# Transposing products of rotated q and k placed one by one between the products with v, and the maxima transposed as fp32r

## The chip, the cores and the metric

The kernel runs on one core of a Trainium2 chip. The metric is the device time of one execution in microseconds. TensorE is written PE, VectorE DVE, ScalarE ACT, GpSimd POOL, SyncE SP, as in the profile; PEld are PE's weight loads.

## The reference, cut to what matters

The kernel is one transformer layer on 16 batch elements of 256 tokens by 128 features: modulated layer norm, attention with 16 query heads, 4 key and value heads and rotary embedding, a residual, then a second modulated layer norm and a two-layer MLP with binarized weights.

```python
h = _layernorm(x) * (1 + ca) + sa
q = (h @ Wq)  -> 16 heads of 64;  k, v = h @ Wkv -> 4 heads of 64
q = q * cos + _rotate_half(q) * sin        # k alike
attn = softmax(q @ k.T * SCALE)
x = x + ga * (attn @ v @ Wo + bo)
h = _layernorm(x) * (1 + cb) + sb
return x + gb * (gelu(h @ bw1 + b1) @ bw2 + b2)
```

## The kernel before, in words

**Stages.** A prologue loads weights and prepares modulation and signs. Then come 18 attention steps (`attention_steps`, L129): one that only prepares, one per batch element, and a tail; then the MLP steps (`mlp_steps`, L143). In an attention step of the steady kind, of which there are 14 (batch elements 1 to 14), three batch elements are in hand: the attention of this one, the output product of the one before, and the normalisation, q, k, v and rotation of the next.

**Slots.** A step has eight slots, one per pair of heads. In each slot PE makes the transposed scores of the pair (`scores`, L942, two chunks of keys, here S0 and S1, two products of 512 columns each), and the product of the previous pair's probabilities with v (`product_with_v`, L958): six products of 512 columns, of high and low parts, in four parts of 2, 2, 1 and 1. Between these stand *units*, listed by hand in `UNITS` (L60) and dealt out one after each S and each part (`slot_order`, L180); what is left over comes at the end of the slot.

**Units.** "xT": transposes of the normalised tokens (2). "qkv c n": 512 columns of q, k, v for token chunk c, three products; n = 2 is k and v, n = 0 and 1 are q. "kt", "qt": the rotated k or q of two heads transposed, four products of 128 columns against an fp32r identity (L907). "s h": row-wise scores of head h, two products of 256 columns, only for the maxima. "mT": the maxima of four heads transposed in fp32. "bc": the reciprocal sums of a pair broadcast to 64 rows each, one product of 256 columns. "yT": the output product, eight fp32 products, in two halves. "zT": back to token rows.

**Who reads a unit.** DVE reads s (the maxima, L728), bc (normalises the pair's output into `o_t`, two instructions, L733), qkv (v_lo at L712, then the two rotation products rot_a and rot_b at L718 and L720), zT (L738); it also makes the low part of the layer norm output from xT (h_lo, L704). ACT reads xT (h_t, h_hi), the v part of qkv (v_hi, L541), kt, qt, mT and yT, and makes the exponentials, two for each S. Rotation goes on from DVE to POOL (rot_sum, L468), ACT (L570) and POOL again (L472).

**Order and waits.** Each engine runs its own list of instructions strictly in order, and every list goes through the units in the same order, `slot_order`. So moving a unit moves its reader's place too, if the units around it have the same reader. DVE has work of its own at fixed slots: statistics ahead of slot 4, normalising ahead of slot 6, the reciprocals of the sums ahead of slots 2 and 5 (L743), and the low part of the probabilities of pairs 0, 2 and 6 at the end of their slots (L827). The units share four PSUM banks in turn (`unit_banks`, L79): a unit waits until the unit four places before it, of the same bank, has been read (`wait_for_reader`, L853).

**The reciprocals.** DVE makes reciprocals with a high and a low part (L746 to L750), SP sends both with two DMAs (L407), and the first bc of the half waits for both to land (L927). The bc of pairs 4 to 7 belong to the batch element before and stand in slots 3 and 4.

Of the kernel before, what the change touches and what calls it, by code (L numbers as in the profile page):

```python
# [178 lines left out]

def slot_order(st, s):  # L180

    held = {"scores": st.attn, "pv": st.attn if s >= 1 else st.out, "un": st.attn if s >= 2 else st.out}
    rest, order = units(st, s), []
    for w in WORK:
        if held[w[0]]:
            order.append((None, w))
            if rest and w[0] in ("scores", "pv"):
                order.append(rest.pop(0))
    return order + rest
# [43 lines left out]
def adaln_layer(nc, x, wq, wkv, wo, bo, w1, b1, w2, b2, c, wmod, cos, sin, out):  # L233
    ctx = ExitStack()
    with ctx:
# [129 lines left out]
        def _(sp):  # L365
            sp.dma_start(c_sb[:, :], c).then_inc(c_in, 16)
            sp.dma_start(xa[:, 0, :, :], x[0].rearrange("(c p) d -> p c d", p=P)).then_inc(x0_in, 16)
            sp.dma_start(wmod_sb[:, :], wmod).then_inc(wmod_in, 16)
# [725 lines left out]
```

## Time and profile before

| | |
|---|---|
| median of 3 runs | 766.95 us (766.94 to 767.4) |
| the profiled execution | 766.3 us, span 764.5 us |
| PE busy | 677.3 us (89%), 3829 instructions |
| DVE busy | 607.1 us (79%), 1275 instructions |
| ACT busy | 592.2 us (77%) |
| POOL busy | 539.4 us (71%) |
| granted TensorE clock, mean | 0.962 |

Times in the rows are microseconds from the span's start. A timeline row gives the start, the length, engine, line, operation, output and inputs; in square brackets the idle time of the engine before it and what ended that. PE's products are pipelined: a row's length holds the fill of the array, so what a product costs is read from the distance between ends of successive rows. The granted clock is 1.00 from 66 to 663 us, which is the upper level, 2.4 GHz.

### The profile page before, as it was taken

How to read it: one execution, taken by the hardware profiler on the slowest of the kernel's cores; microseconds unless marked ns; L12 is line 12 of the kernel's file. 1: busy time of each engine (PE TensorE's matmuls, PEld its weight loads, DVE VectorE, ACT ScalarE, POOL GpSimd, SP SyncE). 2: the span in 40 equal slices, each digit the busy share in tenths (PEclk: the TensorE clock that was granted, in tenths of full speed). 3: DMA queues.
4: the chain of work that ended last, by engine and by line, in shares of the span. 5: the costliest groups of instructions: out<-in, count | busy, mean ns of one | idle time of the engine just before them, and what ended most of it. 6: DMA issues, size and time to landing. Idle time of an engine off the chain costs nothing.

```text
span 764.5 us, 14217 instructions
## 1 busy us (share of the span) xinstructions
PE 677.3 (89%) x3829; PEld 541.3 (71%) x3829; DVE 607.1 (79%) x1275; ACT 592.2 (77%) x1213; POOL 539.4 (71%) x459
## 2 busy tenths in 40 slices
PE   3588999999999999999999999999999999866665
PEld 3465787868777778777777777777778787655654
DVE  6767878787878787888878787878787878549995
ACT  2578988888888888888889888888888888626664
POOL 1568787868696969696877878687878786505564
PEclk9599999999999999999999999999999999978888
DMA  8011111110101111111111101111111111000001
GB/s 234 14 29 30 30 31 30 31 28 18 40 16 28 29 29 29 29 29 29 29 29 29 26 19 29 29 29 29 29 30 30 30 30 30 16 1 17 25 27 42
DMA packets 31578, 24.72 MB, mean 32 GB/s; under 512 B 16688, under 2 KB 26944, under 8 KB 31552
## 3 DMA queue, kind: packets, MB, share of 16 engines
q1 hardware_dynamic: 31552, 24.40, 14.7%
q8 instruction: 13, 0.21, 0.1%
q14 instruction: 13, 0.11, 0.0%
HBM read 4.47 MB, written 2.10 MB: 9 GB/s over the span
## 4 chain that ended last, share of the span: by engine, by line
PE 44%; DVE 21%; issue 18%; ACT 8%; POOL 5%; DMA 1%; DVEq 1%; SPq 0%; POOLq 0%; ACTq 0%
PE o_ps L977 10%; PE unit_ps L934 8%; DVE w_all L728 4%; DVE o_t L733 4%; PE score_ps L952 4%; PE score_ps L954 4%; PE unit_ps L907 4%; PE unit_ps L918 4%; POOL probs_lo L483 3%; DVE recip_hi L748 2%; DVE rot_a L718 2%; DVE rot_b L720 1%; PE unit_ps L928 1%; POOL rot_sum L468 1%; PE unit_ps L891 1%
## 5 line engine op out<-in xcount | busy, mean ns | idle before, releaser
L483 POOL TENSOR_TENSOR probs_lo<-probs,probs_hi 128x512 fp32r<-128x512 f32 x208 | 270.8, 1314 | 51.9 <-ACT probs_hi L622 50.6
L468 POOL TENSOR_TENSOR rot_sum<-rot_a,rot_b 128x512 f32<-128x512 f32 (+1 forms) x96 | 113.2, 1179 | 109.2 <-DVE rot_b L720 108.9
L728 DVE TENSOR_REDUCE w_all<-unit_ps 128x2 f32<-128x512 f32 x256 | 166.4, 683 | 7.9 <-PE unit_ps L918 6.7
L620 ACT ACTIVATE probs<-score_ps 128x512 f32<-128x512 f32 x256 | 150.9, 589 | 3.5 <-PE score_ps L954 3.2
L622 ACT ACTIVATE probs_hi<-score_ps 128x512 fp32r<-128x512 f32 x256 | 152.2, 594 | 0.0
L918 PEld LDWEIGHTS unit_ps<-k_hi,q_hilo 128*128 128x128 f32 x512 | 95.1, 193 | 37.9 <-DVE o_t L733 6.0
L907 PEld LDWEIGHTS unit_ps<-ident_r,qk_rot 128*128 128x128 f32 x640 | 95.7, 194 | 29.4 <-DVE o_t L733 13.3
L733 DVE TENSOR_TENSOR o_t<-o_un,unit_ps 64x256 f32<-64x256 f32 x256 | 106.8, 417 | 8.5 <-PE unit_ps L928 3.8
L952 PE MATMUL score_ps<-q_hilo,k_hi 128*128 128x512 f32 x256 | 108.1, 422 | 2.9 <-DMA q_him<-neg_max_t 1.5
L472 POOL TENSOR_TENSOR qk_rot<-rot_sum,qk_rot 128x512 fp32r<-128x512 f32 (+1 forms) x96 | 105.6, 1106 | 5.2 <-ACT qk_rot L570 5.2
L918 PE MATMUL unit_ps<-k_hi,q_hilo 128*128 128x256 f32 x512 | 106.1, 291 | 2.7 <-DVE rot_b L720 1.4
L907 PE MATMUL unit_ps<-ident_r,qk_rot 128*128 128x128 f32 x640 | 92.7, 269 | 10.9 <-DVE o_t L733 9.0
L977 PE MATMUL o_ps<-probs_lo,v_hi 128*65 128x512 f32 x256 | 101.5, 405 | 0.0
L954 PE MATMUL score_ps<-q_him,k_lo 65*128 65x512 f32 x256 | 101.5, 397 | 0.0
L552 ACT ACTIVATE q_hilo<-unit_ps 128x512 fp32r<-128x512 f32 x128 | 74.3, 595 | 23.2 <-PE unit_ps L907 22.2
L977 PE MATMUL o_ps<-probs_hi,v_hi 128*65 128x512 f32 x256 | 80.2, 394 | 0.0
L977 PE MATMUL o_ps<-probs_hi,v_lo 128*65 128x512 f32 x256 | 79.8, 393 | 0.0
L627 ACT ACTIVATE o_un<-o_ps 65x512 f32<-65x512 f32 x128 | 74.7, 584 | 3.9 <-PE o_ps L977 2.3
L718 DVE TENSOR_TENSOR rot_a<-unit_ps,cos_sb 128x512 f32<-128x512 f32 (+1 forms) x96 | 57.3, 597 | 18.9 <-PE unit_ps L893 18.1
L934 PEld LDWEIGHTS unit_ps<-o_t,wo_sb 128*128 128x128 f32 x512 | 62.6, 196 | 11.0 <-DVE o_t L733 9.6
L934 PE MATMUL unit_ps<-o_t,wo_sb 128*128 128x128 f32 x512 | 65.1, 282 | 4.6 <-DVE o_t L733 4.6
L455 POOL TENSOR_TENSOR rstd<-var_eps,minus_half 128x2 f32<-128x2 f32 x32 | 27.2, 850 | 48.0 <-DVE var_eps L660 48.0
(110 smaller groups left out, 1206.4 us busy)
## 6 DMA issues: line engine op xcount, KB each, us to landing
q_him<-q_hilo SPq DMA_DIRECT2D x64, 256.0 KB
out_x<-w_all SPq DMA_DIRECT2D x16, 128.0 KB, 1.8
xa<-in_L_attn_x SPq DMA_DIRECT2D x3, 640.0 KB, 6.9
q_him<-neg_max_t SPq DMA_DIRECT2D x64, 4.0 KB
w_all<-in_L_attn_Wq SPq DMA_DIRECT2D x1, 512.0 KB, 4.2
w_sb<-in_L_ffn_w SPq DMA_DIRECT2D x2, 256.0 KB, 3.1
wo_sb<-in_L_attn_Wo SPq DMA_DIRECT2D x1, 512.0 KB, 7.5
sums<-o_un SPq DMA_DIRECT2D x32, 8.0 KB, 2.0
```

What stands on the lines that cost most here:

```text
L468: pool.tensor_tensor(total, rot_a[k % 2][:, 0:heads, :], rot_b[k % 2][:, 0:heads, :], ALU.add).then_inc(rot_summed, 1)
L483: pool.tensor_tensor(probs_lo[s % 2][:, jc, :, :], probs[s % 2][:, jc, :, :], probs_hi[s % 2][:, jc, :, :].bitcast(F32), ALU.subtract).the ...
L620: act.activation(probs[s % 2][:, jc, :, :].rearrange("p h i -> p (h i)"), score_ps[jc][:, :], ACT.Exp, scale=SCALE)
L622: act.activation(probs_hi[s % 2][:, jc, :, :].rearrange("p h i -> p (h i)"), score_ps[jc][:, :], ACT.Exp, scale=SCALE).then_inc(probs_read ...
L728: dve.tensor_reduce(neg_max[u[1] // 4][:, first:first + C], ps[:, :].rearrange("p (c j) -> p c j", c=C), AX.X, ALU.max, negate=True).then_ ...
L733: ins = dve.tensor_tensor(o_t[h * DH:h * DH + DH, u[1], :], o_un[0:DH, u[1], h, :], ps[h * DH:h * DH + DH, 0:N], ALU.mult)
L907: ins = pe.matmul(ps[:, h * N + ch * P:h * N + (ch + 1) * P], qk_rot[:, ch, first + h, :, :].rearrange("p t d -> p (t d)"), ident_r[:, :], ...
L918: ins = pe.matmul(ps[:, ch * N:(ch + 1) * N], q_hilo[par][:, h, ch * P:(ch + 1) * P], k_hi2[par][:, g, :], start=True, stop=True)
L934: ins = pe.matmul(ps[:, own], wo_sb[:, s, :], o_t[:, s, own], start=s == 0, stop=s == PAIRS - 1)
L952: pe.matmul(ps[:, :], k_hi2[par][:, g, js], q_hilo[par][:, hs, :].rearrange("p h i -> p (h i)"), start=True, stop=False)
L954: pe.matmul(ps[:, :], k_lo1[par][:, g, js], q_him[s // 2 % 2][:, s % 2 * 2:s % 2 * 2 + 2, :].rearrange("p h i -> p (h i)"), start=False, s ...
L977: ins = pe.matmul(o_ps[i][0:DH + 1, :], v[par][:, jc, g, :], p[i][:, jc, :, :].rearrange("p h i -> p (h i)"), start=part == 0 and jc == 0, ...
```

## The change

`UNITS` is replaced by `SLOTS`, which writes out every slot in full: S0, S1 are the scores, "m" is one single product with v, and a kt, qt, xT or zT stands once for each of its products. The four products of a kt or qt thus stand one by one, most of them each behind an m. The order of the units changes with it; an evicting engine takes a unit at the place of its last product. The maxima get a tile of their own in fp32r, and are transposed by a product with the fp32r identity. `wmod_sb` moves into the memory of `probs[1]`.

```diff
-UNITS = [
-    [("s", 4), ("s", 5), ("s", 6), ("s", 7), ("xT", 0), ("qt", 4), ("mT", 1)],
-    [("qkv", 0, 2), ("s", 8), ("qkv", 1, 2), ("qt", 5), ("s", 9)],
-    [("s", 10), ("s", 11), ("qkv", 0, 0), ("qt", 6), ("mT", 2)],
-    [("s", 12), ("qkv", 1, 0), ("bc", 4), ("bc", 5), ("kt", 0), ("qt", 7)],
-    [("bc", 6), ("bc", 7), ("s", 13), ("s", 14), ("s", 15), ("yT", 0), ("mT", 3)],
-    [("yT", 1), ("kt", 1), ("qkv", 0, 1), ("qt", 0), ("qt", 1)],
-    [("s", 0), ("s", 1), ("s", 2), ("s", 3), ("qkv", 1, 1), ("mT", 0), ("zT", 0)],
-    [("bc", 0), ("bc", 1), ("bc", 2), ("qt", 2), ("qt", 3), ("bc", 3)],
+SLOTS = [
+    "S0 s4 S1 s5 m s6 m s7 m xT0 m xT0 m qt4 m qt4 qt4 qt4 mT1",
+    "S0 qkv02 S1 m qt5 m qt5 m qt5 m qt5 m s8 m qkv12 s9",
+    "S0 s10 S1 s11 m qt6 m qt6 m qt6 m qt6 m qkv00 m mT2",
+    "S0 bc4 S1 bc5 m qt7 m qt7 m qt7 m qt7 m s12 m qkv10",
+    "S0 bc6 S1 bc7 m s13 m kt0 m kt0 m kt0 m kt0 m s14 s15 yT0 mT3",
+    "S0 S1 yT1 m qt0 m qt0 m qt0 m qt0 m qt1 m qt1 qt1 qt1 qkv01",
+    "S0 s0 S1 s1 m s2 m s3 m kt1 m kt1 m kt1 m kt1 qkv11 zT0 zT0 mT0",
+    "S0 bc0 S1 bc1 m qt2 m qt2 m qt2 m qt2 m qt3 m qt3 qt3 qt3 bc2 bc3",
 ]
...
+        neg_max = sb("neg_max", [P, 4, P], F32R)
...
-        neg_max = [w_all[:, 2 * FF + i * P:2 * FF + (i + 1) * P] for i in range(4)]
+        wmod_sb = probs[1][:, :, :, :].rearrange("p c h i -> p (c h i)")[:, 0:6 * D]
...
-                    for h in range(2):
-                        for ch in range(C):
-                            ins = pe.matmul(ps[:, h * N + ch * P:h * N + (ch + 1) * P],
-                                            qk_rot[:, ch, first + h, :, :].rearrange("p t d -> p (t d)"),
-                                            ident_r[:, :], start=True, stop=True)
+                    h, ch = part // 2, part % 2
+                    ins = pe.matmul(ps[:, part * P:(part + 1) * P],
+                                    qk_rot[:, ch, first + h, :, :].rearrange("p t d -> p (t d)"),
+                                    ident_r[:, :], start=True, stop=True)
...
-                    ins = pe.transpose(ps[:, 0:P], neg_max[u[1]], ident[:, :])
+                    ins = pe.matmul(ps[:, 0:P], neg_max[:, u[1], :], ident_r[:, :], start=True, stop=True)
...
-                p, v, chunks = [(probs_hi, v_hi, (0, 1)), (probs_hi, v_lo, (0, 1)),
-                                (probs_lo, v_hi, (0,)), (probs_lo, v_hi, (1,))][part]
-                for jc in chunks:
-                    ins = pe.matmul(o_ps[i][0:DH + 1, :], v[par][:, jc, g, :], p[i][:, jc, :, :].rearrange("p h i -> p (h i)"),
-                                    start=part == 0 and jc == 0, stop=part == 3)
+                p, v = [(probs_hi, v_hi), (probs_hi, v_lo), (probs_lo, v_hi)][part // 2]
+                jc = part % 2
+                ins = pe.matmul(o_ps[i][0:DH + 1, :], v[par][:, jc, g, :], p[i][:, jc, :, :].rearrange("p h i -> p (h i)"),
+                                start=part == 0, stop=part == 5)
```

## Rows read from the trace of the kernel before

**Rows 1.** The page, busy time of each engine.

```profile
PE 677.3 (89%) x3829; PEld 541.3 (71%) x3829; DVE 607.1 (79%) x1275; ACT 592.2 (77%) x1213; POOL 539.4 (71%) x459
```

**Rows 2.** PE timeline about one qt (386.56), the window ending after one, two, four products.

```profile
386.32 0.40 PE L977 MATMUL o_ps<-probs_hi,v_lo 128*65 128x512 f32 x1
386.56 0.22 PE L907 MATMUL unit_ps<-ident_r,qk_rot 128*128 128x128 f32 x1
386.56 0.33 PE L907 MATMUL unit_ps<-ident_r,qk_rot 128*128 128x128 f32 x2
386.56 0.56 PE L907 MATMUL unit_ps<-ident_r,qk_rot 128*128 128x128 f32 x4
```

**Rows 3.** Busy time by stretch (length, PE, PEld, DVE, ACT, POOL, clock, DMA).

```profile
357.82:361.66 3.84, 3.84 (x25) 3.19 (x23) 3.75 (x8) 2.96 (x7) 2.84 (x3) 1.00 0.32 68
361.66:364.66 3.00, 2.54 (x12) 1.79 (x12) 1.03 (x3) 2.97 (x9) 0.00 (x0) 1.00 0.01 1
364.66:379.66 15.00, 14.76 (x80) 11.36 (x78) 14.63 (x33) 13.28 (x28) 13.66 (x13) 1.00 0.15 30
379.66:386.38 6.72, 6.57 (x48) 6.00 (x49) 2.49 (x7) 4.71 (x11) 5.66 (x6) 1.00 0.08 16
386.38:397.35 10.97, 10.35 (x58) 7.67 (x56) 10.55 (x17) 9.48 (x21) 8.77 (x7) 1.00 0.13 26
317.63:397.35 79.72, 76.16 (x437) 60.36 (x436) 65.18 (x131) 66.78 (x140) 61.81 (x53) 1.00 0.14 28
```

**Rows 4.** Waits of DVE in one step, 357.82 to 397.35 (total us, times, longest).

```profile
DVE recip L746 <- DMA sums<-o_un: 3.5, 1, 3.5
DVE v_lo L712 <- ACT v_hi L541: 1.2, 1, 1.2
DVE rot_a L718 <- PE unit_ps L893: 0.9, 2, 0.6
DVE h_lo L704 <- ACT h_hi L539: 0.7, 1, 0.7
```

**Rows 5.** DVE timeline, slots 1 to 3 of that step.

```profile
366.26 0.41 DVE L712 TENSOR_TENSOR v_lo<-unit_ps,v_hi 128x256 fp32r<-128x256 f32 x1
...
368.13 0.97 DVE L748 CAST recip_hi<-recip 128x16 fp32r<-128x16 f32 x1
369.13 0.66 DVE L750 TENSOR_TENSOR recip_lo<-recip,recip_hi 128x16 fp32r<-128x16 f32 x1
...
373.61 0.69 DVE L718 TENSOR_TENSOR rot_a<-unit_ps,cos_sb 128x512 f32<-128x512 f32 x1
```

**Rows 6.** ACT timeline, the second v_hi of slot 1.

```profile
365.80 0.38 ACT L541 ACTIVATE v_hi<-unit_ps 128x256 fp32r<-128x256 f32 x1 [0.21 <-PE unit_ps L893]
```

**Rows 7.** SP timeline, the reciprocals' second DMA of slot 2, and PE's first bc.

```profile
370.54 0.66 SPq L407 DMA_DIRECT2D recip_parts<-recip_lo  x1
...
373.79 0.28 PE L928 MATMUL unit_ps<-recip_parts,select 128*128 128x256 f32 x1
```

**Rows 8.** Timeline of the tail step, where nothing else covers the reciprocals.

```profile
672.48 0.17 DVE L748 CAST recip_hi<-recip 128x16 fp32r<-128x16 f32 x1
...
673.55 0.61 SPq L407 DMA_DIRECT2D recip_parts<-recip_lo  x1
675.51 0.47 PE L928 MATMUL unit_ps<-recip_parts,select 128*128 128x256 f32 x2 [2.48 <-DMA recip_parts<-recip_lo]
```

**Rows 9.** DVE timeline, slot 4.

```profile
377.93 1.73 DVE L733 TENSOR_TENSOR o_t<-o_un,unit_ps 64x256 f32<-64x256 f32 x4
379.70 1.89 DVE L728 TENSOR_REDUCE w_all<-unit_ps 128x2 f32<-128x512 f32 x3
```

**Rows 10.** PE timeline, slots 4 and 5.

```profile
379.81 2.02 PE L934 MATMUL unit_ps<-o_t,wo_sb 128*128 128x128 f32 x16 [0.23 <-DVE o_t L733]
381.67 0.30 PE L922 MATMUL unit_ps<-ident,w_all 128*128 128x128 f32 x1
...
384.54 0.56 PE L907 MATMUL unit_ps<-ident_r,qk_rot 128*128 128x128 f32 x4
...
385.86 0.40 PE L893 MATMUL unit_ps<-w_hi,h_lo 128*128 128x512 f32 x1
```

More of the change, by code:

```diff
@@ L48, with parsed @@
 EPS = 1e-5
-UNITS = [
[8 rows of a table removed]
-]
-ALL_UNITS = [(slot, u) for slot, units in enumerate(UNITS) for u in units]
+SLOTS = [
[8 rows of a table added]
+]
+def parsed(slots):
+    found = []
+    for text in slots:
+        words, slot, product = text.split(), [("un",)], 0
+        for n, word in enumerate(words):
+            kind = word.rstrip("0123456789")
+            number = word[len(kind):]
+            if kind == "S":
+                slot.append(("scores", int(number)))
+            elif kind == "m":
+                slot.append(("pv", product))
+                product += 1
+            else:
+                name = (kind, *map(int, number)) if kind == "qkv" else (kind, int(number))
+                slot.append(("part", name, words[:n].count(word), word not in words[n + 1:]))
+        found.append(slot)
+    return found
+ORDER = parsed(SLOTS)
+ALL_UNITS = [(slot, w[1]) for slot, order in enumerate(ORDER) for w in order if w[0] == "part" and w[3]]
+PLACE = {u: k for k, (_, u) in enumerate(ALL_UNITS)}
 LATE_UNITS = ([("qt", s) for s in range(4, PAIRS)] + [("s", h) for h in range(4, HEADS)] + [("mT", q) for q in range(1, 4)]
@@ L177, in units, with slot_parts @@
     return [(k, u) for k, (s, u) in enumerate(ALL_UNITS) if s == slot and has(st, u)]
+def slot_parts(st, s):
+    held = {"scores": st.attn, "pv": st.attn if s >= 1 else st.out, "un": st.attn if s >= 2 else st.out}
+    return [w for w in ORDER[s] if (has(st, w[1]) if w[0] == "part" else held[w[0]])]
 def slot_order(st, s):
[L182 to L189, printed above, removed]
+    return [(PLACE[w[1]], w[1]) if w[0] == "part" else (None, w)
+            for w in slot_parts(st, s) if w[0] != "part" or w[3]]
 def rotated(st, s, end):
@@ L367, in _ @@
             sp.dma_start(xa[:, 0, :, :], x[0].rearrange("(c p) d -> p c d", p=P)).then_inc(x0_in, 16)
[L368 removed]
+            sp.dma_start(wmod_sb, wmod).then_inc(wmod_in, 16)
             sp.dma_start(w_all[:, 0:INNER], wq).then_inc(wq_in, 16)
@@ L727, in unit @@
                     first = u[1] % 4 * C
-                    dve.tensor_reduce(neg_max[u[1] // 4][:, first:first + C], ps[:, :].rearrange("p (c j) -> p c j", c=C), AX.X,
+                    dve.tensor_reduce(neg_max[:, u[1] // 4, first:first + C], ps[:, :].rearrange("p (c j) -> p c j", c=C), AX.X,
                                       ALU.max, negate=True).then_inc(max_ready, 1)
@@ L873, in wait_for_reader, with unit @@
                     pe.wait_ge(x2_ready, st.count(1, 1, of))
-            def unit(st, place, u):
+            def unit(st, place, u, part, last):
                 kind, ps, par = u[0], unit_ps[bank(st, place)], st.par(ahead(u))
                 before = last_in_bank(st, place)
-                if before and u != ("yT", 1):
+                if before and u != ("yT", 1) and part == 0:
                     wait_for_reader(st, *before)
                 if kind == "xT":
-                    pe.wait_ge(ln_out, st.count(1, 1, 1))
-                    for ch in range(C):
-                        ins = pe.transpose(ps[:, ch * P:(ch + 1) * P], xn[:, ch, :], ident[:, :])
+                    if part == 0:
+                        pe.wait_ge(ln_out, st.count(1, 1, 1))
+                    ins = pe.transpose(ps[:, part * P:(part + 1) * P], xn[:, part, :], ident[:, :])
                 if kind == "qkv":
@@ L936, in unit @@
                 if kind == "zT":
-                    pe.wait_ge(z_ready, st.count(1, 1, -1))
-                    for ch in range(C):
-                        ins = pe.transpose(ps[:, ch * P:(ch + 1) * P], z_sb[:, ch * P:(ch + 1) * P], ident[:, :])
-                ins.then_inc(unit_full, 1)
+                    if part == 0:
+                        pe.wait_ge(z_ready, st.count(1, 1, -1))
+                    ins = pe.transpose(ps[:, part * P:(part + 1) * P], z_sb[:, part * P:(part + 1) * P], ident[:, :])
+                if last:
+                    ins.then_inc(unit_full, 1)
             def scores(st, s, jc):
@@ L1051, in step @@
                 for s in range(PAIRS):
-                    for place, w in slot_order(st, s):
-                        if place is not None:
-                            unit(st, place, w)
+                    for w in slot_parts(st, s):
+                        if w[0] == "part":
+                            unit(st, PLACE[w[1]], *w[1:])
                         elif w[0] == "scores":
```

22 lines of the change are left out of this document (9 added, 13 removed).

## The prediction

> **What bounds the kernel now.** The page's busy times come first: PE 677.3 us of 764.5, DVE 607.1, with PEld at 541.3 [rows 1]. By that PE is the bound, and work taken off it should come off the time. The second view asks whether this holds inside a step. Two steady steps take 79.72 us, 39.86 each, and PE counts 76.16 of them as busy [rows 3]; but a busy row holds the fill of the array, so short stalls hide in it. DVE's busy time does not hide stalls. I cut one step at DVE's waits [rows 4] into four legs [rows 3], and read who holds whom:
>
> - Leg 1, 361.66 to 364.66, 3.00 us: DVE is done with the maxima of slot 0 and waits until layer norm, ACT's exponentials and v_hi of slot 1 are through.
> - Leg 2, 364.66 to 379.66, 15.00 us: slots 1 to 4. DVE is busy for 14.63 of it.
> - Leg 3, 379.66 to 386.38, 6.72 us: from the last bc read to the rotation of qkv01. DVE does 2.49 us of work; PE makes yT0, yT1 and qkv01.
> - Leg 4, 386.38 to 397.35 and on through the 3.84 us ahead of leg 1 (357.82 to 361.66), 14.81 us: slots 5 to 7 and slot 0. DVE is busy for 10.55 of 10.97 and 3.75 of 3.84.
>
> The four sum to 39.53, this step without the loop's branch. So DVE is the bound over 29.8 us of a step, through its strict order of work, and PE and ACT bound it only where they hand DVE the next piece: leg 1, leg 3, and the short wait ahead of qkv11 (the 0.9 us in two parts, the longest 0.6, of [rows 4]). What the change does to these hand-overs decides.
>
> **What it takes from PE.** In a group of four the first product ends 0.06 us after the long product before it (386.72 to 386.78), each later one 0.11 later: four end 0.40 after it [rows 2]. The later ones wait for their own weights; the first's were loaded under 512 columns. A lone product between two m should cost 0.06, four 0.24. Six groups of a step stand quite alone (qt5, qt6, qt7, kt0, qt0, qt2): 6 x 0.15; kt1's last is followed by qkv11, whose 128 columns of weights it can't hide: 0.10; qt4, qt1 and qt3 gain by the first only: 3 x 0.05. Sum 1.15 us a step. The maxima as fp32r: the transpose now ends 0.14 after yT0's last product (379.81 + 2.02 to 381.67 + 0.30 [rows 10]); the shorter one still stands ahead of S0, whose weights then show instead. I put it at nothing, within 0.05 x 4 either way.
>
> Here I weigh a rule. The Trainium skill, "TensorE: Matmul & The Clock Gate", part 3, "The mechanism", says that a weight load overlaps a running product only where it goes to other rows of the array. By it a lone product would cost its load as well, 0.11 as now, and the 1.15 would be nothing; the 0.06 in [rows 2] says otherwise, and I take the row.
>
> **What it does to the legs.** All prices are for one step; a 512-column product costs 0.23 (two between 386.26 [rows 10] and 386.72 [rows 2]), one of 256 half that.
>
> Leg 1. xT's second product stands behind four m instead of five: 0.23 earlier, and h_lo, qkv02 and v_hi with it: -0.23.
>
> Leg 2, first part. qkv12 stood behind S1, s8 and two m; now behind S1, six m, the four qt5 and s8. That is 4 x 0.23 + 0.24 = 1.16 later against qkv02. Its v_hi on ACT already waited for PE by 0.21 [rows 6], and DVE took v_lo as soon as s8 was done (366.26 [rows 5]), with about 0.07 to spare. So v_lo comes 1.1 later: +1.1. Behind it in DVE's list are s9, the reciprocals, s10, s11: all of slot 2 follows, and mT2, now the very last of slot 2, waits for s11's maximum and holds S0 of slot 3.
>
> Leg 2, second part. Before, DVE went from the end of recip_lo (369.79 [rows 5]) through s10, s11, qkv00, the low part and s12 to rot_a of qkv10 at 373.61: 3.82 us, and the landing of the reciprocals was covered, since bc4 came at 373.79, behind qkv10 [rows 7]. Now bc4 is the second thing in slot 3. The tail step shows the bare landing: 1.96 from the issue of the second DMA to PE's bc (673.55 to 675.51 [rows 8]). From recip_lo's end to that issue are 0.75 (369.79 to 370.54 [rows 5, 7]), so bc4 ends 0.75 + 1.96 + 0.36 = 3.07 after recip_lo. PE would be there after 2.2 (s10 and s11 on DVE 1.2, mT2 0.4, S0 and bc4 0.6): a new wait of 0.9. Queued behind it on PE are S1, bc5, six m, qt7, s12 and qkv10: 0.46 + 0.12 + 1.40 + 0.24 + 0.23 + 0.70 = 3.15, and DVE's rot_a another 0.13 later (385.86 + 0.40 to 386.38, [rows 10, 3]). So rot_a starts 6.35 after recip_lo instead of 3.82; but bc4 and bc5, four o_t instructions or 1.73 [rows 9], are by then done, which stood behind it: 6.35 - 3.82 - 1.73 = +0.8.
>
> Leg 3. Two things. yT0 takes the bank of s13, which DVE reads only after bc7; before, its bank was bc7's own. It starts one maximum later, 1.89 / 3 = 0.63, with the step to the first of them 0.7 [rows 9]: +0.7. And qkv01, before which S0, yT1, S1, kt1 and two m stood, is now last: six m, qt0 (0.24) and qt1 (0.06 + 0.28, its three in a row and the load of qkv01's weights) stand before it instead of two m and kt1 (0.40 [rows 10]): 4 x 0.23 + 0.24 + 0.34 + 0.05 - 0.40 = +1.15. DVE has nothing else to do meanwhile (2.49 of 6.72 busy).
>
> Leg 4. DVE's order is the same. kt1 now waits for the reader of s0, which costs PE but not DVE; qkv11 comes a bit before DVE is ready instead of 0.33 after: -0.15. bc2 and bc3 wait for DVE at the end as qt3 and bc3 did.
>
> Other queues: SP's order is unchanged; its DMAs for q and for the maxima of quarter 0 are issued with some 4 us to their use, as before. POOL's order is unchanged, and it has 8 us a step to spare [rows 3]. ACT takes kt0 a slot later and z behind S1's exponentials; neither is waited for longer than DVE's chain.
>
> **The sum.** -0.23 + 1.1 + 0.8 + 0.7 + 1.15 - 0.15 = +3.4 us a step. 14 steps: +47.6. The preparing step, step 0 and step 15 have parts of it (step 0 the two late qkv, 2.2): +3, between 0 and 6. Against the profiled execution of 766.3 us that is 816.9, and the median of the runs, 766.95, lies 0.65 above it: **817 us**.
>
> Bounds. Below: the cast of the reciprocals takes 0.97 and recip_lo 0.66 in the steady step [rows 5], the cast 0.17 in the tail [rows 8], where POOL is idle; if they fall between POOL's instructions, leg 2 loses up to 1.3. If the landing is as short as to be covered, 0.9 more. Then 1.2 a step: 784. Above: lone products at 0.11 add 0.05 for each of the 13 in legs 2 and 3, 0.65, and new collisions of the kind of those two 0.6: 4.65 a step, 837.
>
> **Rivals.**
>
> *PE is the bound after all* (other side). DVE's full stretches would then be slack taken up by PE's pace: units come earlier, DVE starts earlier, and each step gives 1.15. For it: 89% against 79% [rows 1], and PE's waits are short. Against it: DVE's 10.55 of 10.97, in the leg where it would have to start earlier. It decides at qkv01: if DVE's wait ahead of that rotation does not grow by more than PE's gain. 14 x 1.15 = 16: 750.8, say 751. Chance 0.16.
>
> *Lone products don't hide their loads* (the rule above, as a mechanism here): all legs as in my sum, with the 0.65 of the upper bound: 14 x 0.65 = 9 more, 826. The first product of each group in [rows 2] speaks against it. Chance 0.07.
>
> *Only the two late qkv cost.* bc4's landing and s13's bank are covered by DVE's own shift: -0.23 + 1.1 + 1.15 - 0.15 less PE's 1.15: 0.7 a step, 777. Chance 0.06.
>
> *Gain and waits cancel*, the maxima and lone products leaving the time as it is: 767. Chance 0.05.
>
> My forecast: 0.66. **Numbers.** About 0.2% of the time is what a measurement of this kernel tells from no change. Slower: 0.66 + 0.07 + 0.06 = 0.79; same 0.05; faster 0.16. The range goes from 766, which takes in the rivals above and the no-change case, to 837: it leaves out the faster case and some 0.04 beyond its ends.
>
> **What would show it.** In the changed kernel a step should be about 43 us long; DVE's wait for qkv01's rotation should be near 2 us instead of 0.6; a wait of the second v_lo on v_hi of some 0.6 should be new, and one of PE's bc in slot 3 on the reciprocals' DMA of 0.9; yT0 should wait on a maximum (L728), not on o_t; lone fp32r transposes should end 0.06 after the m before them, and PEld's busy time stay as it is. The prediction is wrong if the step is below 39.8, if bc4 never waits on the DMA, or if DVE reaches s0 of slot 6 no later after yT1 than now.

## The result and the profile after

The changed kernel takes 839.64 us (median of 4 runs, 836.8 to 841.01) against 767.17 us before (the median of now 4 runs): a ratio of 1.0932, 95% interval 1.0907 to 1.0957. The direction was forecast; the size was not: 817 us was predicted, and the time lies 2.6 us above the range's upper end of 837. The profiled execution took 836.8 us, span 834.9 us, against a span of 764.5 us.

In the new kernel's line numbers the maxima are L748, o_t L753, the reciprocals L766 to L770, rot_a and rot_b L738 and L740, v_lo L732, kt and qt L926, s L937, mT L941, bc L947, yT L953, qkv L911 to L913, the scores S0 and S1 L972 and L974, the products with v L996. First the page: busy time of each engine and the granted clock in 40 slices; the last row is the clock of the kernel before.

```profile
PE 691.4 (83%) x3829; PEld 558.3 (67%) x3829; DVE 617.5 (74%) x1275; ACT 595.1 (71%) x1213; POOL 534.8 (64%) x459
...
PEclk9789899999999999999999999999999999978886
...
PEclk9599999999999999999999999999999999978888
```

No engine came nearer to being the bound than in [rows 1]: PE fell from 89% to 83%. From the sixth slice on the clock's row is 9 through all the steps, as it was before, because a short fall is lost in a slice of 21 us. The next view, busy time by stretch (columns as in [rows 3]), shows one step cut at the prediction's four legs, then the whole of that step, a second step's leg 3, and the 13 steps in which all marks can be read.

```profile
309.15:311.94 2.79, 2.58 (x12) 1.80 (x12) 1.03 (x3) 2.78 (x8) 0.00 (x0) 1.00 0.01 1
311.94:329.14 17.20, 14.17 (x79) 11.00 (x77) 14.99 (x33) 13.39 (x28) 14.89 (x14) 1.00 0.16 32
329.14:337.65 8.51, 8.23 (x58) 7.42 (x59) 3.27 (x7) 5.35 (x12) 5.21 (x5) 1.00 0.01 1
337.65:352.33 14.68, 12.53 (x71) 9.79 (x70) 14.16 (x24) 11.44 (x24) 10.45 (x8) 1.00 0.18 37
309.15:352.33 43.18, 37.51 (x216) 30.01 (x216) 33.45 (x66) 32.96 (x69) 30.54 (x26) 1.00 0.13 26
...
417.69:427.83 10.14, 9.87 (x58) 9.05 (x59) 3.24 (x6) 5.34 (x12) 5.20 (x5) 0.83 0.01 1
...
85.89:666.22 580.33, 507.50 (x2838) 407.71 (x2836) 435.02 (x845) 437.15 (x899) 397.06 (x338) 0.97 0.12 25
```

The first step is the one that the prediction described: 2.79, 17.20, 8.51, 14.68 against 3.00, 15.00, 6.72, 14.81 in [rows 3], so -0.21, +2.20, +1.79, -0.13; forecast were -0.23, +1.9, +1.85, -0.15. It is 43.18 long, 3.65 more than before, where 3.4 was forecast. But the 13 steps take 580.33 us, 44.64 each, and their mean granted clock is 0.97. The row of 10.14 shows the difference: the same leg 3 with the same instructions, at a clock of 0.83. The same 13 steps of the kernel before, 39.80 each:

```profile
82.62:600.00 517.38, 494.70 (x2837) 392.44 (x2836) 423.01 (x846) 434.63 (x898) 401.78 (x339) 1.00 0.14 28
```

The waits of the undisturbed step (309.15 to 352.33; total us, times, longest) are those named in the forecast:

```profile
DVE recip L766 <- DMA sums<-o_un: 4.1, 1, 4.1
...
DVE v_lo L732 <- ACT v_hi L562: 1.9, 2, 1.2
DVE rot_a L738 <- PE unit_ps L913: 1.7, 3, 1.0
...
PE unit_ps L941 <- DVE neg_max L748: 1.4, 1, 1.4
...
PE unit_ps L947 <- DMA recip_parts<-recip_lo: 0.7, 1, 0.7
...
PE unit_ps L953 <- DVE neg_max L748: 0.2, 1, 0.2
```

v_lo now waits twice, bc4 waits for its DMA, yT0 for a maximum. mT2's wait of 1.4 for s11's maximum is the longest stand of PE in the step. Behind it and bc4's wait lies what the forecast lacked. Busy time by stretch of another step, slots 2 and 3:

```profile
494.46:496.80 2.34, 2.34 (x14) 1.59 (x12) 2.27 (x4) 2.29 (x6) 2.34 (x3) 1.00 0.00 0
496.80:500.60 3.80, 1.78 (x8) 1.29 (x9) 3.63 (x8) 1.78 (x5) 2.66 (x4) 0.98 0.05 5
500.60:504.01 3.41, 3.41 (x14) 2.85 (x13) 1.53 (x4) 2.12 (x4) 3.41 (x4) 0.52 0.00 0
504.01:510.00 5.99, 4.83 (x26) 3.58 (x25) 5.29 (x15) 4.96 (x9) 4.56 (x5) 1.00 0.21 44
```

PE is busy throughout, then for 1.78 of 3.80 us; then its clock is 0.52, the lower level of 1.2 GHz, for 3.41 us, and full again. PE's timeline of slot 3 in the undisturbed step (322) and in this one (501):

```profile
321.87 0.40 PE L996 MATMUL o_ps<-probs_hi,v_hi 128*65 128x512 f32 x1
322.11 0.22 PE L926 MATMUL unit_ps<-ident_r,qk_rot 128*128 128x128 f32 x1
322.17 0.39 PE L996 MATMUL o_ps<-probs_hi,v_hi 128*65 128x512 f32 x1
...
501.46 0.63 PE L996 MATMUL o_ps<-probs_hi,v_lo 128*65 128x512 f32 x1
501.88 0.31 PE L926 MATMUL unit_ps<-ident_r,qk_rot 128*128 128x128 f32 x1
501.99 0.63 PE L996 MATMUL o_ps<-probs_hi,v_lo 128*65 128x512 f32 x1
```

At full clock the lone transposing product ends 0.06 after the product with v (322.27 to 322.33), as forecast, and the next product with v 0.23 later. At half clock the same distances are 0.10 (502.09 to 502.19) and 0.43 (to 502.62). Such a stretch at half clock is called a fall from here on. Ten falls, 37.5 us of half clock in all, lie in the 13 steps of the new kernel, each in another step: seven in leg 2 and three early in leg 3. Nine last 3.41 us and one, in the first of the 13 steps, 6.83. The kernel before has none between 45 and 669 us.

### The profile page after: what moved, and what is told of

Its sections match the earlier page's. It is cut to its first block, busy times and chain, and to the rows that moved or that the text cites. A ratio compares the mean times of both kernels' runs of the same rounds, so it can differ in the third digit from the quotient of the medians.

```text
span 834.9 us, 14265 instructions
## 1 busy us (share of the span) xinstructions
PE 691.4 (83%) x3829; PEld 558.3 (67%) x3829; DVE 617.5 (74%) x1275; ACT 595.1 (71%) x1213; POOL 534.8 (64%) x459
## 4 chain that ended last, share of the span: by engine, by line
PE 50%; DVE 23%; issue 11%; ACT 6%; DMA 4%; POOL 3%; SPq 1%; DVEq 1%; ACTq 0%; POOLq 0%
PE o_ps L996 14%; PE unit_ps L953 8%; DVE o_t L753 5%; DVE neg_max L748 4%; PE unit_ps L926 4%; PE score_ps L972 4%; DMA recip_parts<-recip_lo 4%; PE score_ps L974 3%; PE unit_ps L947 3%; PE unit_ps L937 3%; PE unit_ps L911 2%; DVE rot_b L740 2%; DVE recip_lo L770 2%; DVE xn L687 2%; PE unit_ps L913 2%
## 5 line engine op out<-in xcount | busy, mean ns | idle before, releaser
L504 POOL TENSOR_TENSOR probs_lo<-probs,probs_hi 128x512 fp32r<-128x512 f32 x208 | 267.7, 1302 | 53.4 <-ACT probs_hi L643 51.4
L748 DVE TENSOR_REDUCE neg_max<-unit_ps 128x2 fp32r<-128x512 f32 x256 | 163.2, 683 | 28.7 <-PE unit_ps L937 27.8
L926 PE MATMUL unit_ps<-ident_r,qk_rot 128*128 128x128 f32 x640 | 136.5, 243 | 19.1 <-DVE neg_max L748 16.1
L926 PEld LDWEIGHTS unit_ps<-ident_r,qk_rot 128*128 128x128 f32 x640 | 121.4, 200 | 31.3 <-DVE neg_max L748 21.8
L937 PEld LDWEIGHTS unit_ps<-k_hi,q_hilo 128*128 128x128 f32 x512 | 94.7, 192 | 39.4 <-DVE o_t L753 21.6
L937 PE MATMUL unit_ps<-k_hi,q_hilo 128*128 128x256 f32 x512 | 105.8, 291 | 15.5 <-DVE o_t L753 14.3
L753 DVE TENSOR_TENSOR o_t<-o_un,unit_ps 64x256 f32<-64x256 f32 x256 | 106.9, 417 | 13.2 <-PE unit_ps L947 8.4
L972 PE MATMUL score_ps<-q_hilo,k_hi 128*128 128x512 f32 x256 | 107.7, 421 | 2.2 <-issue 1.4
L974 PE MATMUL score_ps<-q_him,k_lo 65*128 65x512 f32 x256 | 103.3, 404 | 0.0
L996 PE MATMUL o_ps<-probs_hi,v_hi 128*65 128x512 f32 x256 | 97.5, 413 | 0.0
L996 PE MATMUL o_ps<-probs_lo,v_hi 128*65 128x512 f32 x256 | 95.3, 406 | 0.0
L996 PE MATMUL o_ps<-probs_hi,v_lo 128*65 128x512 f32 x256 | 93.1, 412 | 0.0
L738 DVE TENSOR_TENSOR rot_a<-unit_ps,cos_sb 128x512 f32<-128x512 f32 (+1 forms) x96 | 57.3, 597 | 31.5 <-PE unit_ps L913 31.5
L953 PE MATMUL unit_ps<-o_t,wo_sb 128*128 128x128 f32 x512 | 70.4, 296 | 4.4 <-DVE neg_max L748 3.1
L953 PEld LDWEIGHTS unit_ps<-o_t,wo_sb 128*128 128x128 f32 x512 | 67.1, 209 | 8.8 <-DVE neg_max L748 6.0
L591 ACT ACTIVATE qk_rot<-rot_sum 128x512 fp32r<-128x512 f32 (+1 forms) x96 | 52.4, 564 | 19.8 <-POOL rot_sum L489 19.8
```

The costliest lines, as they stand in the source:

```text
L504: pool.tensor_tensor(probs_lo[s % 2][:, jc, :, :], probs[s % 2][:, jc, :, :], probs_hi[s % 2][:, jc, :, :].bitcast(F32), ALU.subtract).the ...
L748: dve.tensor_reduce(neg_max[:, u[1] // 4, first:first + C], ps[:, :].rearrange("p (c j) -> p c j", c=C), AX.X, ALU.max, negate=True).then_ ...
L753: ins = dve.tensor_tensor(o_t[h * DH:h * DH + DH, u[1], :], o_un[0:DH, u[1], h, :], ps[h * DH:h * DH + DH, 0:N], ALU.mult)
L926: ins = pe.matmul(ps[:, part * P:(part + 1) * P], qk_rot[:, ch, first + h, :, :].rearrange("p t d -> p (t d)"), ident_r[:, :], start=True, ...
L937: ins = pe.matmul(ps[:, ch * N:(ch + 1) * N], q_hilo[par][:, h, ch * P:(ch + 1) * P], k_hi2[par][:, g, :], start=True, stop=True)
L953: ins = pe.matmul(ps[:, own], wo_sb[:, s, :], o_t[:, s, own], start=s == 0, stop=s == PAIRS - 1)
```

## The experiments

All are the changed kernel with other lines in `SLOTS`, save one. The table gives the mean of 13 steps, cut at the same marks on DVE's timeline; "full clock" is the mean of the steps without a fall, and "falls" counts the stretches at half clock in the 13 steps. "Full clock" rests on few steps where falls are many: three in the changed kernel and in qkv01 early, one in kt0 in slot 3. (Steps are of two kinds that take turns, with a leg 1 of 2.8 or 3.3 us in the changed kernel.) The ratio is to runs of the kernel before that were taken along with each kernel; their medians lie between 767.17 and 768.98 us. The kernels stand in the order in which they are told; two more orders follow at the end.

| kernel | us | ratio to before (95%) | legs 1, 2, 3, 4 | step | full clock | falls |
|---|---|---|---|---|---|---|
| before | 767.17 | | 3.18, 15.02, 6.71, 14.89 | 39.80 | 39.80 | 0 |
| changed | 839.64 | 1.0932 (1.0907 to 1.0957) | 3.04, 18.06, 8.88, 14.66 | 44.64 | 43.40 | 10 |
| old order | 768.79 | 0.9977 (0.9942 to 1.0012) | 3.18, 15.02, 6.76, 15.00 | 39.96 | 39.85 | 1 |
| old order, lone products | 770.60 | 1.0034 (1.0017 to 1.0051) | 3.03, 15.03, 6.76, 14.82 | 39.64 | 39.64 | 0 |
| new order, groups | 837.88 | 1.0858 (1.0784 to 1.0933) | 3.02, 18.19, 8.84, 14.26 | 44.32 | 43.31 | 9 |
| filled | 830.71 | 1.0813 (1.0770 to 1.0855) | 3.04, 17.74, 8.51, 14.66 | 43.94 | 43.94 | 0 |
| slot 3 old | 807.08 | 1.0459 (1.0386 to 1.0531) | 3.04, 16.49, 8.50, 14.66 | 42.69 | 42.26 | 4 |
| qkv12 early | 821.75 | 1.0663 (1.0623 to 1.0703) | 3.04, 16.16, 9.37, 14.65 | 43.23 | 42.27 | 7 |
| qkv01 early | 822.24 | 1.0675 (1.0641 to 1.0710) | 3.05, 18.40, 7.59, 14.66 | 43.70 | 42.56 | 10 |
| kt0 first | 839.41 | 1.0920 (1.0901 to 1.0938) | 3.05, 17.46, 9.37, 14.65 | 44.52 | 43.49 | 9 |
| kt0 in slot 3 | 830.10 | 1.0774 (1.0729 to 1.0819) | 3.05, 18.53, 7.92, 14.65 | 44.15 | 42.56 | 12 |
| all hand-overs | 812.47 | 1.0546 (1.0470 to 1.0622) | 3.04, 15.03, 9.45, 15.13 | 42.65 | 41.38 | 9 |

**Is it the order, or the products and the tile?** The first kernel keeps the fp32r maxima, their tile and the single products in the list, but writes out the order of before, the groups of four together:

```diff
-    "S0 bc4 S1 bc5 m qt7 m qt7 m qt7 m qt7 m s12 m qkv10",
+    "S0 s12 S1 qkv10 m m bc4 m m bc5 m kt0 kt0 kt0 kt0 m qt7 qt7 qt7 qt7",
...
-    "S0 S1 yT1 m qt0 m qt0 m qt0 m qt0 m qt1 m qt1 qt1 qt1 qkv01",
+    "S0 yT1 S1 kt1 kt1 kt1 kt1 m m qkv01 m m qt0 qt0 qt0 qt0 m qt1 qt1 qt1 qt1 m",
```

> The changed kernel with every unit back at its old place, kt and qt in fours, the products with v grouped as before; what stays of the change is the fp32r transpose of the maxima with its own tile, and the weights' place. Theory (the order of the units is what costs): 767 us, within 2 of the kernel before, a step of 39.9 us, granted clock 1.00. Rival (the fp32r maxima or the moved tiles cost something): above 775. Rival (they gain): below 763.

Measured: 768.79 us, the time of before; its step by stretch (columns as in [rows 3]):

```profile
202.26:205.29 3.03, 2.58 (x12) 1.83 (x12) 1.03 (x3) 3.00 (x9) 0.00 (x0) 1.00 0.01 1
205.29:220.27 14.98, 14.74 (x80) 11.34 (x78) 14.59 (x33) 13.27 (x28) 13.63 (x13) 1.00 0.15 30
220.27:227.02 6.75, 6.60 (x48) 6.04 (x49) 2.50 (x7) 4.71 (x11) 5.67 (x6) 1.00 0.09 18
227.02:242.07 15.05, 14.16 (x81) 10.88 (x79) 14.52 (x24) 12.09 (x26) 11.62 (x9) 1.00 0.18 36
```

So the fp32r maxima and the tile are worth nothing that can be measured, and the loss comes from the order of the list; the lone products, which this kernel takes out as well, are settled by the next two. One of its 13 steps has a fall, in leg 4, which is 16.57 there instead of 15.05: the order of before can draw one too.

The second puts the transposing products one by one into that old order of units; only products with v change their place for it:

```diff
-    "S0 bc0 S1 bc1 m m bc2 m m qt2 qt2 qt2 qt2 m qt3 qt3 qt3 qt3 m bc3",
+    "S0 bc0 S1 bc1 m bc2 m qt2 m qt2 m qt2 m qt2 m qt3 qt3 qt3 qt3 bc3",
```

> The old order of units in every slot, with kt and qt products alone behind an m wherever the order leaves one (17 of the 40 in a step stay behind another). Theory (DVE's list is the bound; lone products save only on PE's stretch from yT0 to qkv11): 0.2 to 0.4 us a step, 761 to 765; granted clock 1.00 in every step. Rival (PE is the bound): 0.9 us a step, 754. Rival (lone products cost something by themselves, as the run with all four hand-overs mended could also be read): above 775.

Measured: 770.6 us, above the 761 to 765 expected. The step is 39.64 instead of 39.80 and no more, though the clock stays up, and nearly all of that is leg 1 (3.18 to 3.03), where xT's second product stands behind one product less with v: the time that lone products save on PE is time that nobody waits for. The rival by which PE is the bound falls with that, and so does my hope of a faster kernel; the 2 us that the 13 steps gain are lost again before and behind them, and what loses them there I have not found.

The third is the mirror of that: the new order with the products in groups of four.

```diff
-    "S0 bc4 S1 bc5 m qt7 m qt7 m qt7 m qt7 m s12 m qkv10",
+    "S0 bc4 S1 bc5 m m m m qt7 qt7 qt7 qt7 m s12 m qkv10",
```

> The changed kernel's order of units, but each kt and qt again as four products in a row, standing where the last of its four stood, with the m ahead of them. Theory (order costs, lone products save PE a little): not faster than the changed kernel, 838 to 860, since 0.15 us per group comes back on the two hand-over legs. Rival (lone products between long ones are what slows PE or takes its clock down): the time falls towards 770, and the granted clock is 1.00 in every step.

Measured: 837.88 us with 9 falls. Lone products are neither the cost nor the cause of the falls.

**Do the falls come from PE standing still?** This kernel keeps the order of the changed one to the letter and gives PE dummy products where it waits:

```diff
+                if st.attn and part == 0 and u in (("s", 14), ("s", 15), ("yT", 0)):
+                    pe.wait_ge(o_un_ready, st.count(8, 3))
+                    for _ in range(3 if u == ("s", 14) else 2):
+                        pe.matmul(o_ps[0][:, :], w_hi[:, 0:P], w_hi[:, 0:512], start=True, stop=True)
...
+                    if u[1] == 2:
+                        for _ in range(8):
+                            pe.matmul(ps[:, P:512], w_hi[:, 0:P], w_hi[:, 0:384], start=True, stop=True)
...
+                    if u[1] == 4 and not st.tail:
+                        for _ in range(6):
+                            pe.matmul(ps[:, N:512], w_hi[:, 0:P], w_hi[:, 0:N], start=True, stop=True)
```

> The changed kernel in its own order, with TensorE given dummy products where it stands still: eight of 384 columns ahead of mT2's wait for s11's maximum, six of 256 ahead of the first bc's wait for the reciprocals' DMA, and three, two and two of 512 ahead of s14, s15 and yT0. They go to unused columns or to an accumulator that is overwritten afterwards, and nothing reads them. Theory (the granted clock falls because TensorE stands still in short pieces at the new waits): the clock is 1.00 through the steady steps, a step is about 43.5 us with legs of 3.06, 17.3, 8.5 and 14.7, and the time falls although TensorE has more work: 820 to 826 us. Rival (the falls come from something else in the new order, such as the mix of short products): the falls to half stay, a step is 44.6 us or longer, 836 to 845 us.

Measured: 830.71 us. Its legs 2 and 3 in one step, and its 13 steps (columns as in [rows 3]):

```profile
308.98:326.68 17.70, 16.90 (x98) 13.89 (x96) 14.90 (x33) 13.37 (x28) 14.99 (x14) 1.00 0.15 31
326.68:335.20 8.52, 8.52 (x61) 7.65 (x61) 3.26 (x7) 5.35 (x12) 5.26 (x5) 1.00 0.01 1
...
85.93:657.20 571.27, 530.22 (x3111) 434.39 (x3109) 434.18 (x845) 435.20 (x899) 398.77 (x338) 1.00 0.13 26
```

All ten falls are gone, and every step has a leg 3 of 8.4 to 8.5, though PE now counts 530 us as busy where it had 507. So the falls hang on PE's standing still at these places: with the stands filled they end. The 13 steps are 9.06 us shorter (580.33 to 571.27). The time did not come down to the 820 to 826 expected, because the filling itself costs. The maxima of s10 and s11 on DVE, and PE's rows behind them (here the dummy products are L946 and L954, mT L948, bc L957):

```profile
315.30 1.28 DVE L748 TENSOR_REDUCE neg_max<-unit_ps 128x2 fp32r<-128x512 f32 x2
...
316.03 1.66 PE L946 MATMUL unit_ps<-w_hi 128*128 128x384 f32 x8 [0.80 <-DVE neg_max L748]
317.53 0.22 PE L948 MATMUL unit_ps<-ident_r,neg_max 128*128 128x128 f32 x1
...
318.10 0.87 PE L954 MATMUL unit_ps<-w_hi 128*128 128x256 f32 x6
318.81 0.28 PE L957 MATMUL unit_ps<-recip_parts,select 128*128 128x256 f32 x1
```

The eight products ahead of mT2 use its bank, which s10 had, so they start only when s10's maximum is read, and they last beyond s11's: mT2 starts 0.95 after the end of the second maximum (316.58 to 317.53), where it had started 0.05 after it. The six products ahead of bc4 then come too late for the wait that they were to fill: bc4 ends 3.71 after recip_lo instead of 3.12, and leg 2 is 17.70 instead of 17.20. With that 0.5 a step taken off, the falls cost some 9 + 13 x 0.5 = 15.6 us; from the table it is 13 x (44.64 - 43.40) = 16.1.

The Trainium skill, "TensorE: Matmul & The Clock Gate", section "A second HAM failure mode: psum-queue depth-cycling", tells of a kernel in which PE, idling briefly between groups of products, has its clock swing between the two levels, and puts the loss down to the swing. This case agrees: the 3.80 us in which PE was busy for 1.78 stand ahead of the 3.41 us at 0.52, and the kernel in which the standing is filled has no fall.

**The four hand-overs, one by one.** Each of the next kernels puts one of them back. Slot 3, so that bc4 stands behind qkv10 again:

```diff
-    "S0 bc4 S1 bc5 m qt7 m qt7 m qt7 m qt7 m s12 m qkv10",
+    "S0 s12 S1 qkv10 m bc4 m qt7 m bc5 m qt7 m qt7 m qt7",
```

> The changed kernel with slot 3 alone in the old order: s12 and qkv10 first, then bc4 and bc5 between the products with v (qt7 stays alone). Theory: PE's wait for the landing of the reciprocals goes, leg 2 loses 1.0 us a step, that is 14 us; and if the falls of the granted clock in slot 3 come from PE standing still twice in a row (1.6 us for the maxima, 0.9 us for the landing), they go as well, another 10: 812 to 826. Rival (the landing wait only moves time that DVE's order takes anyway): 836 to 841.

Measured: 807.08 us, 5 under the range expected. A step at full clock is 1.14 shorter (43.40 to 42.26), and six of the ten falls are gone with PE's stand ahead of bc4; mT2's wait of 1.4 is still there. The expectation had both parts, 14 and 10 us, and both held: 13 x 1.14 = 15, and for the falls 13 x ((44.64 - 43.40) - (42.69 - 42.26)) = 10.5. Together they make 25.5 of the 26.2 us by which the profiled executions differ (836.8 and 810.57). The medians differ by 32.6, because the profiled execution was the fastest of four in the changed kernel and the slowest of four here.

qkv12 back to the second place of slot 1:

```diff
-    "S0 qkv02 S1 m qt5 m qt5 m qt5 m qt5 m s8 m qkv12 s9",
+    "S0 qkv02 S1 s8 m m qkv12 m qt5 m qt5 m qt5 m qt5 s9",
```

> The changed kernel with slot 1 alone in the old order (s8, then qkv12 behind two m, qt5 alone behind it). Theory: the second v_lo is 1.1 us earlier again, 15 us; PE's wait for the maxima ahead of slot 3 falls from 1.6 to 0.5 us, and with it the falls of the granted clock in slot 3, another 8 to 13: 810 to 818. Rival (no fall of the clock hangs on that wait): 822 to 826.

Measured: 821.75 us, above the 810 to 818 expected. The term itself held: v_lo to v_lo is 1.60 again instead of 2.70, and a step at full clock is 1.13 shorter. mT2's wait for the maximum is gone, bc4's for its DMA is not (0.6). But the falls moved; busy time by stretch, legs 2 and 3 of two steps:

```profile
307.04:323.17 16.13, 14.31 (x78) 10.94 (x76) 14.98 (x33) 13.39 (x28) 14.94 (x14) 1.00 0.17 34
323.17:331.67 8.50, 8.22 (x58) 7.41 (x59) 3.29 (x7) 5.34 (x12) 5.21 (x5) 1.00 0.01 1
...
393.46:409.60 16.14, 14.31 (x78) 10.93 (x76) 15.02 (x33) 13.37 (x28) 14.95 (x14) 1.00 0.17 34
409.60:419.70 10.10, 9.82 (x58) 8.85 (x59) 3.62 (x7) 5.50 (x12) 5.22 (x5) 0.83 0.01 1
```

Leg 2 has none any more, and leg 3 has one in seven of 13 steps, each worth 1.6. So leg 2 had no fall with bc4's wait alone, and four with mT2's alone (slot 3 old).

qkv01 ahead of qt0 in slot 5:

```diff
-    "S0 S1 yT1 m qt0 m qt0 m qt0 m qt0 m qt1 m qt1 qt1 qt1 qkv01",
+    "S0 S1 yT1 m m qkv01 m qt0 m qt0 m qt0 m qt0 qt1 qt1 qt1 qt1",
```

> The changed kernel with qkv01 alone moved forward in slot 5, behind two m. Theory: leg 3 falls by 1.5 us, leg 4 gives back 0.3 since DVE then waits for qkv11: 1.15 us a step, 16 us; the few falls of the clock in slot 5 go too: 816 to 824. Rival (DVE has slack there): 835 to 841.

Measured: 822.24 us, in the range expected, but not by its parts: leg 3 in steps without a fall is 7.48, 1.03 less instead of 1.5, leg 4 gives nothing back, and there are still ten falls. DVE's timeline of it shows why it is not less:

```profile
331.47 0.25 DVE L766 RECIPROCAL recip<-sums 128x16 f32<-128x16 f32 x1 [4.08 <-DMA sums<-o_un]
331.76 0.97 DVE L768 CAST recip_hi<-recip 128x16 fp32r<-128x16 f32 x1
332.76 0.18 DVE L770 TENSOR_TENSOR recip_lo<-recip,recip_hi 128x16 fp32r<-128x16 f32 x1
332.95 0.69 DVE L738 TENSOR_TENSOR rot_a<-unit_ps,cos_sb 128x512 f32<-128x512 f32 x1
```

rot_a no longer waits for PE; it comes right behind the reciprocals, and these wait for the landing of the sums. That is the next bound of leg 3.

The bank of yT0 took two tries. The first moved s13 behind kt0, so that yT0 takes another bank:

```diff
-    "S0 bc6 S1 bc7 m s13 m kt0 m kt0 m kt0 m kt0 m s14 s15 yT0 mT3",
+    "S0 bc6 S1 bc7 m kt0 m kt0 m kt0 m kt0 m s13 m s14 s15 yT0 mT3",
```

> The changed kernel with kt0 ahead of s13 in slot 4, so that yT0 takes the bank of kt0 instead of s13's. Theory: yT0 waits for the last o_t and not for a maximum: 0.5 us a step, 829 to 834. Rival (the bank did not matter, or kt0's reader on ACT is as late): 836 to 845.

Measured: 839.41 us, not the 829 to 834 expected; leg 3 at full clock is 8.5 as in the changed kernel. In its waits yT0 is now held by the reader of kt0:

```profile
PE unit_ps L953 <- ACT k_lo L570: 2.9, 14, 0.2
```

The second moves kt0 out of slot 4, and yT0 has bc7's bank again:

```diff
-    "S0 bc4 S1 bc5 m qt7 m qt7 m qt7 m qt7 m s12 m qkv10",
-    "S0 bc6 S1 bc7 m s13 m kt0 m kt0 m kt0 m kt0 m s14 s15 yT0 mT3",
+    "S0 bc4 S1 bc5 m qt7 m qt7 m qt7 m qt7 m s12 m qkv10 kt0 kt0 kt0 kt0",
+    "S0 bc6 S1 bc7 m s13 m m m m m s14 s15 yT0 mT3",
```

> The changed kernel with kt0's four products moved from slot 4 to the end of slot 3, so that yT0 again takes the bank of bc7, which DVE reads before s13, as in the kernel before. Theory (the bank term of the prediction, +0.7 us a step, is real, and the earlier try only put another late reader in the maximum's place): leg 3 falls from 8.5 to 7.8 us in steps without a fall of the granted clock, yT0's wait is on o_t (L753) again, and the time is about 829 us, between 824 and 833, as far as falls of the clock do not change. Rival (the bank never mattered, yT0 is held by PE's own queue ahead of it): leg 3 stays at 8.5, 836 to 841 us.

Measured: 830.1 us, as expected. Busy time by stretch of its legs 2 and 3:

```profile
313.21:331.86 18.65, 16.16 (x81) 12.57 (x79) 14.89 (x33) 13.27 (x28) 13.77 (x13) 0.91 0.15 30
331.86:339.78 7.92, 7.78 (x56) 7.19 (x57) 3.28 (x6) 5.53 (x12) 6.41 (x6) 1.00 0.01 2
```

Leg 3 is 7.92, 0.6 less: the bank term is real. But it is not yT0's bank alone. With kt0 behind s13, s14 and s15 had come to the banks of bc6 and bc7. PE's rows of s15 and yT0 in the changed kernel (329), and of s14, s15 and yT0 here (330):

```profile
329.20 0.50 PE L937 MATMUL unit_ps<-k_hi,q_hilo 128*128 128x256 f32 x2 [0.38 <-DVE o_t L753]
329.92 2.05 PE L953 MATMUL unit_ps<-o_t,wo_sb 128*128 128x128 f32 x16 [0.22 <-DVE neg_max L748]
...
330.50 1.03 PE L937 MATMUL unit_ps<-k_hi,q_hilo 128*128 128x256 f32 x4
332.00 2.02 PE L953 MATMUL unit_ps<-o_t,wo_sb 128*128 128x128 f32 x16 [0.47 <-DVE o_t L753]
```

In the changed kernel s15 stands behind the last o_t, and yT0 behind s15 and a maximum; here s14 and s15 are done before, and yT0 is held by that o_t and nothing else. In the first try s15 still waited for the last o_t (0.39). How the 0.6 divides between s15's bank and yT0's no run shows. Twelve of 13 steps have their fall, all in leg 2.

**Can both kernels be beaten?** Three orders were tried, besides the old one with lone products. The first mends all four hand-overs; the edits in slots 4 and 5:

```diff
-    "S0 bc6 S1 bc7 m s13 m kt0 m kt0 m kt0 m kt0 m s14 s15 yT0 mT3",
-    "S0 S1 yT1 m qt0 m qt0 m qt0 m qt0 m qt1 m qt1 qt1 qt1 qkv01",
+    "S0 bc6 S1 m kt0 m kt0 m kt0 m kt0 bc7 m s13 m s14 s15 yT0 mT3",
+    "S0 yT1 S1 m m qkv01 m qt0 m qt0 m qt0 m qt0 qt1 qt1 qt1 qt1",
```

> Lone products kept wherever an m is at hand, but qkv12, qkv10 with bc4 and bc5, and qkv01 as early as in the kernel before, and yT0 again in the bank of bc7. Theory (four late hand-overs are the whole loss, and lone products save only what is not waited for): 755 to 767, granted clock 1.00 in every step, legs near 3.1, 15.0, 6.3 and 14.9 us. Rival (PE is the bound once the hand-overs are mended): the full 1.15 us a step, 748 to 752. Rival (lone products cost something by themselves): above 775.

Measured: 812.47 us, not the 755 to 767 expected. That is in the range of the rival by which lone products cost something by themselves, but the old order with lone products, at 770.6, had none of that cost. Leg 2 is the old 15.03, but I made a wait of my own: s15 takes the bank of kt0, whose reader on ACT is late.

```profile
PE unit_ps L937 <- ACT k_lo L570: 33.6, 15, 2.9
```

The second puts every hand-over earlier than before; slots 1 and 5 of it:

```diff
-    "S0 qkv02 S1 m qt5 m qt5 m qt5 m qt5 m s8 m qkv12 s9",
+    "qkv02 mT1 S0 s8 qkv12 S1 m m m qt5 m qt5 m qt5 m qt5 s9",
...
-    "S0 S1 yT1 m qt0 m qt0 m qt0 m qt0 m qt1 m qt1 qt1 qt1 qkv01",
+    "S0 mT3 yT1 qkv01 S1 m qt0 m qt0 m qt0 m qt0 m qt1 m qt1 qt1 qt1",
```

> Lone products kept, but every hand-over put earlier than in the kernel before: xT's products and qkv02 ahead of slot 1's scores, qkv12 between S0 and S1, qkv01 right behind yT1 and ahead of slot 5's S1, mT3 in slot 5, kt1 late in slot 6. Theory (the order of hand-overs alone sets the step, and lone products leave PE free enough to make them earlier): leg 1 with the start of leg 2 loses about 1.4 us, leg 3 about 1.3, so a step is 37 us instead of 39.8 and the time 725 to 745 us. Rival (PE or a new wait takes what the hand-overs give): a step stays at 39 us or more, 757 us or above.

Measured: 792.99 us, ratio 1.0307 (1.0276 to 1.0337), far above the 725 to 745 expected; a step of 41.25 without a fall. Its waits show PE held 17 times by the reader of a qt whose bank an s takes:

```profile
PE unit_ps L937 <- ACT q_hilo L573: 16.5, 17, 1.2
```

The third goes from the old order with lone products and moves two things:

```diff
-    "S0 s4 S1 s5 m s6 m s7 m xT0 m xT0 m qt4 m qt4 qt4 qt4 mT1",
+    "S0 s4 S1 s5 m s6 m xT0 xT0 s7 m m m qt4 m qt4 qt4 qt4 mT1",
...
-    "S0 yT1 S1 m kt1 m kt1 kt1 kt1 qkv01 m qt0 m qt0 m qt0 m qt0 qt1 qt1 qt1 qt1",
+    "S0 yT1 S1 qkv01 m m kt1 m kt1 kt1 kt1 m qt0 m qt0 m qt0 qt0 qt1 qt1 qt1 qt1",
```

> The order of the kernel before with lone products (the earlier run of 39.7 us a step), and two hand-overs put earlier, each past work that nobody waits for: xT's products ahead of s7 in slot 0, and qkv01 ahead of kt1 and two m in slot 5. Theory (DVE's hand-overs set the step, and a bank or a clock fall must not be traded for them): qkv01's rotation starts 0.8 us earlier and leg 1 loses about 0.5, so a step is 38.3 to 38.8 us and the time 745 to 758 us. Rival (ACT, which is busy through leg 1, or PE takes what they give): a step of 39.4 us or more, 764 us or above.

Measured: 786.43 us, ratio 1.0230 (1.0201 to 1.0259), not the 745 to 758 expected. Legs 1 and 3 fall by 0.6 each, but leg 4 grows by 2.5 (14.82 to 17.31, with two falls in the 13 steps), and the step is 40.95. Again an s waits for q_hilo (8.3 us in 14 waits), and in the 13 steps DVE waits 13.3 us for an s on PE, which it did not in the old order with lone products; how the whole 1.3 a step comes about I have not worked out. No order that I tried beats the kernel before.

## Why the prediction was right and wrong

**The bound.** Right: DVE's hand-overs set the step. With the same PE work in the old order the time is that of before; with lone products there the step moves by 0.16.

**The terms at full clock.** Leg 1: -0.23 forecast, -0.21 measured. qkv12: +1.1 forecast; v_lo to v_lo went from 1.60 to 2.70, and putting it back gave 1.13. bc4's landing: +0.8 forecast; rot_a comes 6.39 after recip_lo's end in the undisturbed step (forecast 6.35), and the old slot 3 gave 1.14 back, 0.3 more than the term. Leg 3: +1.85 forecast, +1.79 measured, of it 0.6 for the banks (0.7 forecast, for yT0's alone; s15's bank had been overlooked) and 1.03 for qkv01 (1.15 forecast), which the landing of the sums cuts short. Leg 4: -0.15 forecast, -0.13 measured. In the mean of the steps without a fall that is 43.40 - 39.80 = +3.6, for 3.4 forecast. (The last addition, 816.9 and 0.65, gives 817.6 rather than 817.)

**The step that failed** is the sum's price for PE's work: "a 512-column product costs 0.23" was carried through all legs at the granted clock of 1.00 that the kernel before has between 66 and 663 us. The prediction found the two new stands of PE in slots 2 and 3, named the queue behind them, and priced only the wait. In ten of 13 steps the wait, or the one ahead of s14, s15 and yT0, was followed by 3.4 us or more at half clock. A fall of 3.41 us made its leg 1.2 to 1.6 us longer, the one of 6.83 us 2.6. In the 13 steps that is 16.1 us, and without it the time would have been near 824, inside the range. Nothing in the bounds above (0.65 for the lone products, 0.6 for collisions) was of this kind, and no rival was.

The span grew by 70.4 us where 50.6 were forecast. 13 steps account for 62.95: 13 x 3.6 = 46.8 at full clock and 16.1 by the falls; 3.3 lie ahead of them and 4.2 behind. So of the 19.8 missing, 16.1 are the clock, 2.6 the 0.2 a step, the rest the ends. The median lies another 2.8 above the profiled execution.

**The rivals.** PE as the bound, with its 751 us, falls by the old order with lone products. The rule that lone products don't hide their loads falls by the 0.06 that they take at full clock. The case that only two late qkv cost falls by the old slot 3 and the moved kt0. That gain and waits cancel falls by the time itself.

**The signs.** Right: a step of 43 (where the clock holds), the second v_lo's wait (0.66 of the 1.9), bc4 on the DMA (0.7 for 0.9), yT0 on a maximum, 0.06 for a lone product, PEld per step (30.01 for half of 60.36 in [rows 3]). Wrong: DVE's wait for qkv01 is 1.03, not 2, because the reciprocals ahead of it in DVE's list wait longer themselves, 4.1 instead of the 3.5 of [rows 4].
